# Choice of experts begun six steps sooner in the attention stage, with its input fetched ahead of a projection's stores and the setup events moved

## The reference

```python
x = x + xattn(layernorm(x), ctx, ctx, Wq, bq, Wk, bk, Wv, bv, Wo, bo)
# ffn, on layernorm(x):
q   = (x_norm @ wq).reshape(B, T, 8, 2, 128)
sim = einsum('bthpd,hkpd->pbthk', q, keys)            # 64 keys a half
s1, i1 = top_k(sim[0], 16);  s2, i2 = top_k(sim[1], 16)
all_scores = s1[..., :, None] + s2[..., None, :]      # 256 pairs
final_scores, pk = top_k(all_scores, 16)              # 16 experts a head
hidden = gelu(einsum('btd,bthkd->bthk', x_norm, expert_down[final_idx]))
hidden = hidden * relu(final_scores)
out = einsum('bthk,bthkd->btd', hidden, expert_up[final_idx])
```

## Time and profile before

| | before |
|---|---|
| median of 3 runs | 1231.68 us (1228.96 to 1233.51) |
| the profiled execution: time | 1229.27 us |
| its span in the trace | 1227.5 us |
| mean granted TensorE clock | 0.917 |
| busy: PE / DVE / ACT / POOL | 1040.2 / 951.9 / 395.9 / 624.2 us |
| slots with scores (first to last reduction) | 38.6 to 438.3 us |
| last task of the choice before the barrier | about 508 us |

### The profile page before, as it was taken

How to read it: one execution, slowest core, us unless ns; L and a number is a source line. 1 busy time by engine, 2 the same in 40 slices (tenths; PEclk the granted TensorE clock), 3 DMA queues, 4 the chain that set the end, 5 groups by cost and what they waited for, 6 DMA issues and landing times.

```text
span 1227.5 us, 28748 instructions
## 1 busy us (share of the span) xinstructions
PE 1040.2 (85%) x10088; PEld 726.1 (59%) x10088; DVE 951.9 (78%) x4836; ACT 395.9 (32%) x725; POOL 624.2 (51%) x776
## 2 busy tenths in 40 slices
PE   4789977877878784158998999999999999999998
PEld 2434433323212222047787787888878888888887
DVE  4757554969999998688999999898988989953310
ACT  2247644434444362023222222222222222222211
POOL 6330420332211322226777778787867696877511
PEclk9799988888879797557999999999999999999999
DMA  5344213221221100260000000010000010000000
GB/s 171 117 149 143 94 57 119 63 78 50 87 89 45 48 11 24 84 266 3 1 30 16 16 25 21 16 34 16 26 12 25 2 34 16 26 15 25 2 18 9
DMA packets 60353, 63.89 MB, mean 52 GB/s; under 512 B 7185, under 2 KB 56593, under 8 KB 59697
## 3 DMA queue, kind: packets, MB, share of 16 engines
q1 hardware_dynamic: 60208, 62.03, 15.6%
HBM read 42.34 MB, written 19.66 MB: 51 GB/s over the span
## 4 chain that ended last, share of the span: by engine, by line
PE 53%; DVE 28%; POOL 7%; issue 7%; DMA 3%; ACT 2%; SPq 1%; DVEq 0%; POOLq 0%; ACTq 0%
PE bank L1299 50%; DVE mem L1218 4%; PE bank L1302 3%; POOL mem L804 2%; DVE mem L1154 2%; DVE mem L1101 2%; DVE mem L1100 2%; DVE mem L1255 2%; DVE mem L1105 1%; DVE mem L1097 1%; DVE mem L1150 1%; DVE mem L1157 1%; DVE mem L1109 1%; DVE mem L1137 1%; DVE mem L1021 1%
## 5 line engine op out<-in xcount | busy, mean ns | idle before, releaser
L1299 PE MATMUL bank<-mem 128*128 128x32 bf16 (+5 forms) x9608 | 989.9, 276 | 113.2 <-DVE mem L1218 41.2
L1299 PEld LDWEIGHTS bank<-mem 128*128 128x128 bf16 (+4 forms) x9608 | 672.7, 123 | 378.8 <-issue 165.1
L804 POOL TENSOR_TENSOR mem<-mem 128x1536 bf16<-128x1536 bf16 x118 | 325.7, 2761 | 159.0 <-DVE mem L1252 154.5
L1218 DVE TENSOR_REDUCE mem<-bank 128x1 f32<-128x512 f32 x256 | 168.2, 683 | 78.6 <-PE bank L1299 78.4
L924 ACT ACTIVATE mem<-bank 128x512 f32<-128x512 f32 x256 | 149.0, 601 | 199.7 <-PE bank L1299 198.8
L1255 DVE TENSOR_TENSOR mem<-mem,bank 128x2048 bf16<-128x2048 bf16 x128 | 155.4, 1214 | 0.0
L1302 PE MATMUL bank<-mem 128*128 128x128 f32 (+3 forms) x480 | 76.7, 292 | 70.7 <-POOL mem L706 25.0
L1302 PEld LDWEIGHTS bank<-mem 128*128 128x128 f32 (+3 forms) x480 | 56.0, 144 | 119.0 <-issue 76.1
L811 POOL TENSOR_TENSOR mem<-mem 128x512 f32<-128x512 f32 x64 | 83.6, 1306 | 50.5 <-ACT mem L963 50.5
L974 ACT COPY mem<-bank 128x512 f32<-128x512 f32 x128 | 74.9, 585 | 105.2 <-PE bank L1299 105.2
L1252 DVE TENSOR_TENSOR mem<-mem,bank 128x512 bf16<-128x512 bf16 x128 | 52.7, 411 | 67.9 <-PE bank L1299 58.9
(11 more groups left out here) (104 smaller groups left out, 778.1 us busy)
## 6 DMA issues: line engine op xcount, KB each, us to landing
mem<-parts_d SPq DMA_DIRECT2D x192, 64.0 KB, 2.3
parts_d<-mem SPq DMA_DIRECT2D x16, 384.0 KB, 3.1
mem<-in_L_ffn_expert_down SPq DMA_DIRECT2D x16, 256.0 KB, 2.9
downT_d<-mem SPq DMA_DIRECT2D x16, 256.0 KB, 3.1
mem<-downT_d SPq DMA_DIRECT2D x4, 1024.0 KB, 8.7
mem<-in_L_ffn_expert_up SPq DMA_DIRECT2D x4, 1024.0 KB, 16.4
tok_d<-mem SPq DMA_DIRECT2D x16, 160.0 KB, 1.8
mem<-tok_d SPq DMA_DIRECT2D x16, 160.0 KB, 2.4
```

Of the source, the lines that this page charges most:

```text
L804: nc.gpsimd.tensor_tensor(ow[q % 2], i0, i1, ALU.mult).then_inc(ow_rdy, 1)
L1218: nc.vector.tensor_reduce(nmx[g % 2][:, i % TB, i // TB:i // TB + 1], psum[n % 3][:, :], AX.X, ALU.max, negate=True).then_inc(s_max, 1)
L1299: return nc.tensor.matmul(o, l, r, start=first, stop=last)
```

## The change

`AHEAD` = 6 moves each tile's tasks: before, searches, choosing, keys and extraction of a tile lay at steps 5 to 30 of its two slots (spread over 27 steps); after, they are spread over 28 steps beginning at step -2. Counted from the start of the tile's first slot, the tasks go

| | search | choose | keys | extract |
|---|---|---|---|---|
| before | 5, 6, 8, 9, 11, 12, 14, 16 | 17, 19, 20, 22 | 24 | 25, 27, 28, 30 |
| after | -2, -1, 1, 2, 4, 6, 7, 9 | 11, 12, 14, 16 | 17 | 19, 21, 22, 24 |

The two `sim` events go from steps 1 and 2 of the tile's first slot to steps 11 and 12 of the slot before it; `tok` stays. `yT` goes from steps 6 and 8 to 3 and 5; `wqT`, `kyT`, `wqk` from 9, 10, 15 to 4, 6, 10. On SP the fetch of `xs` moves, in slots with r = 1, ahead of `store_parts`; in slots with r = 3 it stays where it was. No instruction is added or removed, and POOL's loop is untouched.

```diff
+        AHEAD = 6
+
         choice = {}
         for _t in range(NA):
-            for _s, _, _kind, _i in spread(1, 5, 32):
-                choice.setdefault((choice_start(_t) + _s // 16, _s % 16), []).append((_t, _kind, _i))
+            for _s, _, _kind, _i in spread(1, 4, 32):
+                _at = 16 * choice_start(_t) - AHEAD + _s
+                choice.setdefault((_at // 16, _at % 16), []).append((_t, _kind, _i))
...
             if r == 3 and b >= 1:
-                ev += [(6, "yT", (b - 1, 0)), (8, "yT", (b - 1, 1))]
-            if g % 2 == 0 and g >= choice_start(0):
-                tile = (g - choice_start(0)) // 2
-                if tile < NA:
-                    ev += [(1, "sim", (tile, 0)), (2, "sim", (tile, 1))]
-                if 1 <= tile <= NA:
-                    ev.append((6, "tok", tile - 1))
+                ev += [(3, "yT", (b - 1, 0)), (5, "yT", (b - 1, 1))]
+            tile = (g + 1 - choice_start(0)) // 2
+            if g == choice_start(tile) - 1 and 0 <= tile < NA:
+                ev += [(17 - AHEAD, "sim", (tile, 0)), (18 - AHEAD, "sim", (tile, 1))]
+            if g == choice_start(tile) and 1 <= tile <= NA:
+                ev.append((6, "tok", tile - 1))
             if g < JL // 2:
                 ev.append((7, "down", g))
             if g < HP // 2:
-                ev += [(9, "wqT", g), (10, "kyT", g), (15, "wqk", g)]
+                ev += [(4, "wqT", g), (6, "kyT", g), (10, "wqk", g)]
...
+            def fetch_sim_input(tile):
+
+                for e in range(2):
+                    sp.wait_ge(xn_wr[e], 16 * (tile // TB + 1))
+                load_sim_input(tile)
+
...
                 load_setup(g + 2)
+                tile = (g + 1 - choice_start(0)) // 2
+                if r == 1 and g == choice_start(tile) - 1 and 0 <= tile < NA:
+                    fetch_sim_input(tile)
                 if r == 1 and b + 1 < B:
                     for n in range(4):
                         store_parts(b + 1, n)
...
-                tile = (g + 1 - choice_start(0)) // 2
-                if g == choice_start(tile) - 1 and 0 <= tile < NA:
-                    for e in range(2):
-                        sp.wait_ge(xn_wr[e], 16 * (tile // TB + 1))
-                    load_sim_input(tile)
+                if r == 3 and g == choice_start(tile) - 1 and 0 <= tile < NA:
+                    fetch_sim_input(tile)
```

## The result

The changed kernel took 1247.72 us (median of 4 runs, 1245.06 to 1252.94), the kernel before 1230.32 (median of 4 runs beside it): ratio 1.0148, 95% interval 1.0102 to 1.0195, so 17.4 us or 1.5% slower. The forecast was 1242, slower, with a range to 1250. The profiled execution took 1247.52 us with a span of 1245.7; against 1229.27 before that is 18.2 us more, which the two traces now have to account for.

What follows compares the result with a forecast made beforehand. It took DVE's work plus its idle time as the bound from slot 8 on. Terms 5.2 - 7.8 + 2.0 + 12.0 + 0.3 = +11.7 us gave 1241.0 profiled, 1243.4 on the median, taken as 1242; range 1232 to 1250.

Steps and rivals of the forecast that it cites:

- (d): Rival: PE's clock drops as it idles, so similarities take 1.5 us more for tiles 1 to 4, +6: 1248; chance 0.12.
- What bounds the kernel: From slot 8 on, the time is DVE's work, which the change leaves as it is, plus DVE's idle time.
- The new wait: Slots 10, 14 and 18: DVE waits about 4.6 us at choose for POOL's candidate sums; +12.0 us net, bounds +8 and +14.
- Tile 0: Slots 7 and 8: input still lands at 201.74, PE idles some 9 us, DVE work is deferred; +5.2 us, bounds +3 and +7.
- Tile 1: Slots 9 and 10: earlier fetch cuts DVE's idle time from 11.8 to 4.0 us; -7.8 us, bounds -10 and -4.
- Tile 2: Slot 11: PE arrives about 14 us in, input lands at 16.5 to 17.5; +2 us, bounds 0 and +4.
- Tiles 3 and 4, and the tail: Slots 13 and 15: similarities should cost the 1.5 us of before, 0; the second stage should take what it took.
- The events: Moved setup events: kyT frees SP, up to -0.5; wqk ahead of o, up to +0.9; +0.3 us, bounds -2 and +2.
- the shared port: DVE and POOL contend for SBUF: moving keys to slot 9's step 1 could give back or cost 0.9 us; not summed.
- (b): Rival: PE and ACT set the pace of slots 9 to 16 and hide DVE's new stalls, 1222; chance 0.08.
- (c): Rival: starved stretches shrink more, tile 0's input lands sooner and tile 2 finds its input; +4.5, 1236; chance 0.20.

Runs made afterwards that it cites:

- e1: The changed kernel with the second half of POOL's candidate sums moved to the head of a tile's first slot: 1238.14 us, ratio 1.0073 to the kernel before.
- e2: The changed kernel with tile 0 alone begun as late as before, its similarities at steps 1 and 2 of slot 8: 1244.62 us, ratio 1.0142.
- e3: The changed kernel with the fetch for tiles 2 and 4 moved up to right behind the stacks: 1240.63 us, ratio 1.0097.
- e4: The kernel before with only the events yT, wqT, kyT and wqk moved as in the change: 1232.85 us, ratio 1.0028.
- e7: The changed kernel with POOL's shift_x alone moved from slots with r = 3 to those with r = 2: 1242.49 us, ratio 1.0105.
- e8: The changed kernel with yT back at its old steps everywhere and wqT, kyT, wqk back except in slot 7: 1247.75 us, ratio 1.0158.
- e5: The changed kernel with the edits of e1, e2 and e3 together and all moved events back at their old steps: 1223.46 us, ratio 0.9957.
- e6: The kernel of e5 with POOL's shift_x also moved from slots with r = 3 to those with r = 2: 1221.58 us, ratio 0.9937.
- e10: The kernel before with POOL's shift_x alone moved from slots with r = 3 to those with r = 2: 1227.15 us, ratio 0.9988.

## Why the prediction was right, and where it was short

The sign, the mechanism and the largest term held; the sum was 11.7 us where the profiled executions differ by 18.2. The measured 1247.7 lies near the upper end of the range. That end had been left open for the clock (rival (d), 1248), and most of what was missing came from elsewhere, so that the time lies inside it is in part luck.

- **What bounds the kernel** (DVE's work plus its idle time): the ledger above closes on it, and e1, e2 and e3 each took away the idle time that they were aimed at. The premise that the change leaves DVE's work as it is failed by 2.7 us of busy time.
- **The new wait** (+12.0, the largest term): three waits of 4.43, 4.43 and 4.42 us for the candidate sums, expected 4.6, and 1.27, 1.27 and 1.87 at the first norm. 17.7 us in all, where the kernel before had 5.9: +11.8. e1 removed the waits at `choose` and with them 9.0 of it.
- **Tile 0** (+5.2): +6.4 of idle time in slots 7 and 8; e2 took 6.3 of it back. The step "its input lands at 201.74 as before" was wrong by 2.8 us: it landed at 204.58. 1.7 of this is the later start of slot 7. The other 1.2 comes from the moved events, since e4 has it too: three more of them now stand ahead of `down`, and SP waits for that before its loads and stores (the second store of xn_d went out at 198.13 for 193.02; it was fetched again after 3.9 us instead of 6.2, which gave 2.3 back). The relay starts 3.4 us into the slot instead of 2.5, but SP stood for `down` later on in any case. I had looked only at what `yT` gates, not at what it stands ahead of. "PE idles some 9 us" was wrong too: it was 6.11, because PE was slower on its way through slot 7 (DVE waited 2.84, 2.06 and 2.19 us for it there), so the sum of this term came out nearer than its parts.
- **Tile 1** (-7.8): 11.6 us of idle DVE became 4.1 (0.67, 2.77 and 0.68), -7.5. The forecast of 4.0 left was right in this execution; 1.7 to 4.5 in other kernels with the same order there say that so close a hit is luck.
- **Tile 2** (+2.0, bounds 0 and +4): mis-sized. It was +5.9 (5.14, 1.46 and 0.68 for 1.4 before), outside the bounds. PE reached the similarities 14.2 us into the slot, as worked out, but the input landed at 18.7, not at 16.5 to 17.5. The step that failed is "at most a us sooner by the earlier `yT`": SP waits for `down` in this slot and not for `yT`, and the fetch went out 15.4 us into it for 14.7. Half a us of that goes with the long cast at the head of the slot (14.9 in e7); the relay has no part in it (15.2 in e8, where it is on time). And a PE idle for 4.62 us took 8.70 us over 24 matmuls at a granted clock of 0.75, where similarities before had taken 5.88 over 21 at 1.00. That is rival (d) at one tile, and e3 shows that it goes with the late input.
- **Tiles 3 and 4, and the tail** (0): about 1.2 us less idle time than before.
- **The events** (+0.3, bounds -2 and +2): slots 0 to 6 took 2.3 us more in the profiled execution and e4 was 3.4 us slower. The failing step was to count events and not banks: with two banks in turn, one more event at step 4 made its neighbour wait for DVE. e8 shows the other side, 4.7 us in slot 15 that `yT` saved, which I had not seen either; with the fetch moved up (e3, e5) it is no longer needed.
- **Left out of the sum**: the shared port. The forecast told the rule and put it at plus or minus 0.9 us for `keys`. It was 4.3 us at another place, two casts of 2.31 us. The new order let POOL's 2.40 us addition begin just ahead of DVE's cast, whereas before it ran at 309.19, well inside slot 11 and with no such cast beside it. `keys` of tile 0 gave back 0.65, as the rule had it. I had applied the rule to the one row in which it showed and not to the instructions that would get new neighbours.

Rivals: (b), hidden stalls, fell with e1. (c) fell too, since neither tile 0's nor tile 2's input landed sooner. (d) was partly true, for tile 2; for tile 1 PE's granted clock was 1.00 (262 to 271), and behind tiles 3 and 4 DVE waited 0.7 and 1.3 us, so that (d)'s number, 1248, is met by chance. Of the 6.5 us that were missing from the sum, tile 2's input gives 3.9, the casts less `keys` about 3.6, the events 2, tile 0 1.2; against that stand tiles 3 and 4 with the tail (1.2), 1.5 less behind the last task, 0.6 less ahead of slot 0, and 0.9 less of DVE's busy time elsewhere, which I can't place. What stays open is why slots 3 and 5 are 1.5 us longer in some executions than in others with the same order of events, and why DVE's idle time in slot 9 was 4.3 and 4.7 us in two kernels and 1.9 to 3.0 in others with the same order there.

## What to carry to other kernels

When a step is moved in a hand-written order, look on every engine that feeds it for what now stands ahead of the feeding instruction: here a wait of 4.4 us came from a POOL loop that the change did not touch, and most of it could be had back by moving one call there. Ask of each moved event not only what it lets start but what it now stands ahead of (here `down`, for which SP waited) and what it shares a bank with. Check an input's landing time against the moment at which its reader gets there before moving the reader: for tile 0 and tile 2 the reader came to a closed door, and only tile 1, whose input could come sooner, gained much. Measure the smallest part of a change by itself: the fetch alone gained 3 us, while the whole change cost 17 and, with its side effects mended, was not measurably better than the fetch alone.

## What the runs showed of the hardware

A small DVE instruction can be long because of POOL, and the profile then shows it as busy and not as a wait. A cast of 128x16 took 2.31 us beside a POOL addition of 2.40 us that had begun 0.12 us earlier, and 0.16 when that addition ran elsewhere; a tensor_scalar of 128x256 took 2.4 instead of 0.41 in slot 6 for the same reason (it, too, was short again in e6, e7 and e10), instructions of `keys` 0.86 to 1.50 instead of 0.57, and max and match-replace instructions beside POOL's longer ones kept their length within 0.02 us. This is how the Trainium skill ("SBUF — State Buffer", section "Who interferes with whom") puts it, copies, casts and tensor_scalar contending through their 2-port modes, whoever issues first blocking the other; the runs agree. An estimate of the size, from each instruction's length less the usual length of its form where POOL ran beside it, is 3 to 11 us of DVE's busy time in each of these kernels up to the last task. DVE busy time that rises though the instructions are the same (here by 2.7 us) is the sign to look for.
